# Rotary attention: scores as plain float32 products of 64 rows in the two row halves of the array

## The reference

```python
qkv = xn @ w_qkv                                   # xn: twice normalized x, (2, 1024, 128)
q, k, v = heads(q), heads(k), heads(v)             # (2, 16, 1024, 64)
q = concat([q[:, :, :1], rope(q[:, :, 1:])])       # rope(t) = t * cos + rot(t) * sin
k = concat([k[:, :, :1], rope(k[:, :, 1:])])
dots = einsum('bhqd,bhkd->bhqk', q, k) * 64 ** -0.5
out = einsum('bhqk,bhkd->bhqd', softmax(dots), v)
x = x + out.reshape(2, 1024, 1024) @ w_out
```

## Time and profile before

| | us |
|---|---|
| median of 3 runs | 1244.94 (1240.4 to 1246.34) |
| profiled execution, device time | 1243.7 |
| its span, first to last instruction | 1241.8 |
| row maxima of the rotary attention, first to last start | 36.6 to 721.7 |
| mean granted TensorE clock | 0.926 of 2.4 GHz |

### The profile page before, as it was taken

How to read it: one execution, slowest core, us unless ns; L and a number is a source line. 1 busy time by engine, 2 the same in 40 slices (tenths; PEclk the granted TensorE clock), 3 DMA queues, 4 the chain that set the end, 5 groups by cost and what they waited for, 6 DMA issues and landing times. The chain is left out here.

```text
span 1241.8 us, 33787 instructions
## 1 busy us (share of the span) xinstructions
PE 1087.8 (88%) x13139; PEld 724.9 (58%) x13139; DVE 920.9 (74%) x1385; ACT 765.4 (62%) x1393; POOL 508.5 (41%) x299
## 2 busy tenths in 40 slices
PE   3799999999999999999999975937999999999876
PEld 1466666666666666666666664935744555445434
DVE  6888888888888889888888964445866665567326
ACT  4577777677777767777777736523256555456633
POOL 0466865675586567658656705730000000000000
PEclk8899999999999999999999985968589988889986
DMA  5866566555656655565666524122451110110001
GB/s 159 212 152 153 141 142 146 140 137 127 156 140 137 146 146 141 123 154 135 137 146 152 138 87 141 53 73 94 145 180 43 53 53 18 36 53 19 2 7 34
DMA packets 63338, 138.14 MB, mean 111 GB/s; under 512 B 12737, under 2 KB 33122, under 8 KB 59186
## 3 DMA queue, kind: packets, MB, share of 16 engines
q1 hardware_dynamic: 61426, 132.87, 42.1%
q0 software_dynamic: 1856, 4.52, 1.2%
HBM read 62.77 MB, written 22.41 MB: 69 GB/s over the span
## 5 line engine op out<-in xcount | busy, mean ns | idle before, releaser
L566 ACT ACTIVATE a_probs<-a_score,a_negmax 128x1024 f32<-128x1024 f32 x256 | 285.5, 1115 | 185.3 <-DVE a_negmax L668 182.6
L668 DVE TENSOR_REDUCE a_negmax<-a_score 128x1 f32<-128x1024 f32 x256 | 310.0, 1211 | 91.5 <-PE a_score L444 91.5
L1586 DVE TENSOR_REDUCE a_lowest<-a_score 128x1 f32<-128x512 f32 (+3 forms) x320 | 181.7, 629 | 84.3 <-PE a_score L1474 46.7
L1556 ACT ACTIVATE a_probs_T<-a_score_T 128x1024 f32<-128x1024 f32 (+1 forms) x192 | 146.7, 810 | 136.9 <-PE a_score_T L1450 93.9
L674 DVE STREAM_TRANSPOSE a_probs_Tb<-a_probs 128x1024 f32<-128x1024 f32 x128 | 156.9, 1226 | 0.1
L674 DVE STREAM_TRANSPOSE a_probs_Ta<-a_probs 128x1024 f32<-128x1024 f32 x128 | 156.9, 1226 | 0.0
L401 POOL TENSOR_TENSOR residual<-residual,a_scaled 128x512 f32<-128x512 f32 x62 | 79.3, 1290 | 146.3 <-ACT a_scaled L582 146.3
L444 PE MATMUL a_score<-a_k_stackbh,a_q_stackb 128*128 128x512 f32 x256 | 113.6, 444 | 25.1 <-ACT a_probs L566 25.1
L444 PE MATMUL a_score<-a_k_stackah,a_q_stacka 128*128 128x512 f32 x256 | 119.3, 466 | 17.1 <-DMA a_q_stacka<-a_q_lo 14.5
L456 PE MATMUL a_acc<-a_probs_Tb,a_v_repb 32*64 32x256 f32 x4096 | 127.8, 384 | 2.3 <-ACT a_scaled L582 2.3
L456 PE MATMUL a_acc<-a_probs_Ta,a_v_repa 32*64 32x256 f32 x4096 | 126.9, 380 | 0.0
(11 more groups left out here) (248 smaller groups left out, 1886.8 us busy)
## 6 DMA issues: line engine op xcount, KB each, us to landing
shared<-shared SPq DMA_DIRECT2D x136, 128.0 KB, 2.3
a_v_repa<-rows_v SPq DMA_DIRECT2D x64, 256.0 KB, 4.5
a_v_repb<-rows_v SPq DMA_DIRECT2D x64, 256.0 KB, 5.0
a_xn_cur<-normed_T SPq DMA_DIRECT2D x17, 512.0 KB, 3.4
rows_v<-a_v_stage SPq DMA_DIRECT2D x68, 128.0 KB, 2.4
a_k_stackah<-a_k_stackah SPq DMA_DIRECT2D x16, 256.0 KB, 2.9
a_k_stackal<-a_k_stackal SPq DMA_DIRECT2D x16, 256.0 KB, 2.9
a_q_stacka<-a_q_lo SPq DMA_DIRECT2D x16, 256.0 KB, 2.9
```

The costliest lines, as they stand in the source:

```text
L566: nc.scalar.activation(probs[s % 2][:], score_ps[s % 2][:], ACT.Exp, bias=negmax[:, s:s + 1], accum_out=den[:, s:s + 1]).then_inc(probs_re ...
L668: nc.vector.tensor_reduce(negmax[:, s:s + 1], score_ps[s % 2][:], axis=AX.X, op=ALU.max, negate=True)\
L1556: nc.scalar.activation(probs_T[k % 4][:, 2 * hp:2 * hp + 2, 0:hi - lo], score_T_ps[n % 2][:, :, 0:hi - lo], ACT.Exp).then_inc(pair_free, 1)
L1586: nc.vector.tensor_reduce(to, src, axis=AX.X, op=ALU.max, negate=True).then_inc(bank_free, 1)
```

## The change

The split is gone. q and k are used as the plain float32 that `total` leaves in `turned`:

- `q_twice[h]` holds the 64 rows of head h in both halves of the partitions; `k_halves[h]` holds keys 0 to 511 in partitions 0 to 63 and keys 512 to 1023 in partitions 64 to 127. SyncE places both by four DMAs for each head (`place`), straight from `turned`.
- A score tile is two float32 products of 64 rows and 512 columns. Each uses one row half of the array and writes its own PSUM bank.
- `high_part` and `rest` are removed, and with them two ScalarE and two GpSimd instructions for each head, and those of ScalarE and VectorE ahead of the loop.
- `total` now waits until both heads' operands of the pair before have been placed. `place_next(h, pairs)` waits for both totals, and through `rden_ready[h]` for the end of head h's scores. `rden_ready` is split by head.
- GpSimd's loop has a new order: both `add_group`s, both `scale`s, both `total`s.

```diff
-        q_lo = sb("q_lo", [P, N], F32R)
-        q_stack = [sb(f"q_stack{h}", [P, N], F32R) for h in "ab"]
-        k_stack = [[sb(f"k_stack{h}{part}", [P, N], F32R) for part in ("h", "l")] for h in "ab"]
+        q_twice = [sb(f"q_twice{h}", [P, N]) for h in "ab"]
+        k_halves = [sb(f"k_halves{h}", [P, N // 2]) for h in "ab"]
...
+                def place(h, i):
+                    own = slice(64 * h, 64 * h + 64)
+                    for c in range(2):
+                        to, cols = (q_twice[h], slice(0, N)) if i == 0 else (k_halves[h], slice(c * N // 2, c * N // 2 + N // 2))
+                        sp.dma_start(to[64 * c:64 * c + 64, :], turned[i][own, cols]).then_inc(operands_placed[h], 16)
...
-                def stack(h, pairs):
-                    sp.wait_ge(hi_ready[h][1], pairs)
-                    copy_rows(k_stack[h][0], k_stack[h][0], h)
-                    sp.wait_ge(lo_ready[h][1], pairs)
-                    copy_rows(k_stack[h][1], k_stack[h][1], h)
-                    sp.wait_ge(lo_ready[h][0], pairs)
-                    copy_rows(q_stack[h], q_lo, h)
+                def place_next(h, pairs):
+                    sp.wait_ge(summed[0], pairs)
+                    sp.wait_ge(summed[1], pairs)
+                    sp.wait_ge(rden_ready[h], pairs)
+                    for i in range(2):
+                        place(h, i)
...
                 def total(i, p):
                     pool.wait_ge(rotated[i], count(p, 2, 2))
+                    for h in range(2):
+                        pool.wait_ge(operands_placed[h], count(p, PLACED, 0))
                     nc.gpsimd.tensor_tensor(turned[i][:], raw[i][:], rot[i][:], ALU.add).then_inc(summed[i], 1)
...
-                        now, p, later = (it, 0), (it, 1), (it, 2)
-                        pool.wait_ge(summed[1], count(p, 1, 1))
+                        now, later = (it, 0), (it, 2)
                         pool.wait_ge(added, count(now, 4, 2))
-                        for i in (1, 0):
-                            rest(0, i, p)
-                        pool.wait_ge(lo_ready[0][0], count(p, 1, 1))
                         add_group(0, now, batch)
-                        scale(0, later)
-                        pool.wait_ge(rotated[0], count(later, 2, 2))
-                        for i in (1, 0):
-                            rest(1, i, p)
-                        pool.wait_ge(lo_ready[1][0], count(p, 1, 1))
-                        total(0, later)
-                        scale(1, later)
-                        total(1, later)
                         add_group(1, now, batch)
+                        for i in range(2):
+                            scale(i, later)
+                        for i in range(2):
+                            total(i, later)
...
                     for half in range(2):
-                        cols = slice(half * 512, half * 512 + 512)
-                        for part in range(2):
-                            last = nc.tensor.matmul(score_ps[s % 2][:, cols], q_stack[h][:, tile * P:tile * P + P],
-                                                    k_stack[h][part][:, cols], start=part == 0, stop=part == 1)
+                        rows = slice(64 * half, 64 * half + 64)
+                        last = nc.tensor.matmul(score_ps[s % 2][:, half * 512:half * 512 + 512], q_twice[h][rows, tile * P:tile * P + P],
+                                                k_halves[h][rows, :], start=True, stop=True)
...
                         if s == TB - 1:
-                            pe.wait_ge(stacked[1], count(p, STACKED, STACKED))
+                            pe.wait_ge(operands_placed[1], count(p, PLACED, PLACED))
                         if s == SLOTS - 1:
-                            pe.wait_ge(stacked[0], count(p, STACKED, 2 * STACKED))
+                            pe.wait_ge(operands_placed[0], count(p, PLACED, 2 * PLACED))
...
-                    if s in (10, 11) and not last:
-                        i = 11 - s
-                        act.wait_ge(summed[i], count(p, 1, 2))
-                        act.wait_ge(scores_ready, count(p, SLOTS, TB))
-                        high_part(0, i)
-                    if s in (1, 2) and not (first or tail):
-                        act.wait_ge(scores_ready, count(p, SLOTS, 0))
-                        high_part(1, 2 - s)
```

More of the change, by code:

```diff
@@ L195, in rotary_attention @@
         summed = [sem("q_summed"), sem("k_summed")]
-        hi_ready = [[sem(f"{n}_hi_{h}_ready") for n in "qk"] for h in "ab"]
-        lo_ready = [[sem(f"{n}_lo_{h}_ready") for n in "qk"] for h in "ab"]
-        stacked = [sem("a_stacked"), sem("b_stacked")]
+        operands_placed = [sem("a_operands_placed"), sem("b_operands_placed")]
         v_stored, v_loaded = sem("v_stored"), [sem("v_a_loaded"), sem("v_b_loaded")]
@@ L201, in rotary_attention @@
         item_ready, item_kept = sem("item_ready"), sem("item_kept")
-        pv_done, attn_kept, rden_ready, projected, out_kept, added = (sem(n) for n in ("pv_done", "attn_kept", "rden_ready", "projected", "out_kept", "added"))
-        STACKED, V_PARTS, ITEMS = 48, 64, 6
+        pv_done, attn_kept, projected, out_kept, added = (sem(n) for n in ("pv_done", "attn_kept", "projected", "out_kept", "added"))
+        rden_ready = [sem("rden_a_ready"), sem("rden_b_ready")]
+        PLACED, V_PARTS, ITEMS = 64, 64, 6
         ITEM_SLOTS = {14: (2, (0,)), 15: (2, (1,)), 0: (1, (2, 3)), 6: (1, (4,)), 7: (1, (5,))}
@@ L255, in load_wo @@
                         sp.dma_start(wo_cur[h][64 * half:64 * half + 64, :], w_out[rows, :]).then_inc(wo_loaded[h], 16)
-                def copy_rows(to, src, h):
-                    own, other = slice(64 * h, 64 * h + 64), slice(64 - 64 * h, 128 - 64 * h)
-                    sp.dma_start(to[other, :].bitcast(F32), src[own, :].bitcast(F32)).then_inc(stacked[h], 16)
+                def place(h, i):
[3 more added lines that the diff above has]
+                        sp.dma_start(to[64 * c:64 * c + 64, :], turned[i][own, cols]).then_inc(operands_placed[h], 16)
                 def store_v(rows):
@@ L299, in _ @@
                 load_weights(slice(P, 2 * P))
-                stack(0, 1)
-                stack(1, 1)
+                for i in range(2):
+                    sp.wait_ge(summed[i], 1)
+                    place(0, i)
+                for i in range(2):
+                    place(1, i)
                 sp.wait_ge(item_kept, ITEMS)
@@ L325, in _ @@
                     q_kept, k_kept, v_kept = (count(q, ITEMS, k) for k in (2, 4, 6))
-                    stack(0, pairs)
+                    place_next(0, pairs)
                     sp.wait_ge(pv_done, a_valued)
@@ L337, in _ @@
                     swap_halves(1)
-                    stack(1, pairs)
+                    place_next(1, pairs)
                     sp.wait_ge(pv_done, b_valued)
@@ L386, in total @@
                     pool.wait_ge(rotated[i], count(p, 2, 2))
+                    for h in range(2):
+                        pool.wait_ge(operands_placed[h], count(p, PLACED, 0))
                     nc.gpsimd.tensor_tensor(turned[i][:], raw[i][:], rot[i][:], ALU.add).then_inc(summed[i], 1)
-                def rest(h, i, p):
-                    rows = slice(64 * h, 64 * h + 64)
-                    pool.wait_ge(hi_ready[h][i], count(p, 1, 1))
-                    nc.gpsimd.tensor_tensor((q_lo, k_stack[h][1])[i][rows, :], turned[i][rows, :], (q_stack[h], k_stack[h][0])[i][rows, :].bitcast(F32),
-                                            ALU.subtract).then_inc(lo_ready[h][i], 1)
                 def add_group(h, p, batch):
@@ L546, in _ @@
                 pe.wait_ge(item_kept, 4)
-                pe.wait_ge(stacked[0], STACKED)
+                pe.wait_ge(operands_placed[0], PLACED)
                 scores(0)
@@ L567, in exponentials @@
                                          accum_out=den[:, s:s + 1]).then_inc(probs_ready, 1)
-                def high_part(h, i):
-                    rows = slice(64 * h, 64 * h + 64)
-                    nc.scalar.activation((q_stack[h], k_stack[h][0])[i][rows, :], turned[i][rows, :], ACT.Copy).then_inc(hi_ready[h][i], 1)
                 def keep_attention():
@@ L651, in _ @@
                     keep_item(k, first_bank(k))
-                for i in range(2):
-                    act.wait_ge(summed[i], 1)
-                    for h in range(2):
-                        high_part(h, i)
                 act.wait_ge(negmax_ready, 1)
@@ L736, in _ @@
                     rotate_first(i)
-                for h in range(2):
-                    rows = slice(64 * h, 64 * h + 64)
-                    for i, to, high in ((1, k_stack[h][1], k_stack[h][0]), (0, q_lo, q_stack[h])):
-                        dve.wait_ge(hi_ready[h][i], 1)
-                        nc.vector.tensor_tensor(to[rows, :], turned[i][rows, :], high[rows, :].bitcast(F32), ALU.subtract).then_inc(lo_ready[h][i], 1)
                 dve.wait_ge(scores_ready, 1)
```

11 lines of the change are left out of this document (7 added, 4 removed).

## The result

| | before | changed |
|---|---|---|
| median, same chip, 4 runs each | 1243.63 us | 1323.49 us (1321.4 to 1333.55) |
| ratio, 95% interval | 1 | 1.0659 (1.0598 to 1.072) |
| profiled execution, span | 1243.7, 1241.8 | 1324.14, 1322.3 |
| first row maximum starts | 36.63 | 33.55 |
| loop, first to last row maximum | 685.1 | 776.6 |

The period is the distance of the first row maxima of two pairs. The time is 6.6% longer, 20 us above the point of 1303 and inside the range of 1270 to 1345. The loop is 91.5 us longer: 14 x 6.15 = 86.1 in pairs 1 to 14, 1.7 in pair 0, 3.7 in the last.

The account below looks back on a forecast made before the run. VectorE and TensorE were both taken as close to the bound. Profiled 1243.7 + 48 (stall) + 14 (clock) - 3.8 (ahead of the loop) = 1301.9; the median lies 1.2 above that execution, so 1303 us, range 1270 to 1345.

Parts of the forecast that it names:

- The mechanism: TensorE in slot 15: a stall of about 3.4 us that carries through every pair, 48 us over 14 pairs; chance 0.80.
- Score tile: Scores on TensorE: two float32 products side by side take 1.05 us, 0.07 less a tile.
- The rival of halves not side by side: Score products on TensorE: row halves don't overlap fully, tile 1.48 us, program about 1350 to 1358; chance 0.08.
- Stretch to slot 7: From a pair's first scores to slot 7's scaling end: 26.76 us, change taken as zero, bounds -0.6 and +0.7.
- The count of seven: TensorE, from a pair's first scores to slot 7: seven switches of tile shape, +0.7 us together.
- the price of 0.1: TensorE, between scores and neighbours of another tile shape: each switch estimated at about 0.1 us.
- GpSimd: GpSimd behind slot 7's scaling: one add and six long instructions, totals ready 15.5 us later.
- Placing: SyncE's four DMAs behind the totals: issues 1.45, landing 2.9, semaphores 0.1, together 4.45 us; bounds 3.85 and 6.55.
- The range's high end: Likeliest case over 14 pairs: 14 x (3.4 + 0.7 + 1.2 + 1.0) = 88, so 1329; 1354 with the clock at its bound.
- Clock: TensorE around slot 15's stall: falls to 1.2 GHz cost 1.0 us a pair, bounds 0 and 2.8; 14 us in all.
- the rival's place: Slots 8 to 10, only scores left: clock falls again after the stall's fall; 1328 and more, to 1365; chance 0.08.
- Ahead of the loop: Between k's total and the first scores: about 3.1 us where 6.9 were, saving 3.8 us.

Follow-up runs that it names:

- Experiment 1: Changed kernel with GpSimd adding head b's rows behind the rotation again, as before the change; ratio 1.0105 to the kernel before.
- experiment 2: Changed kernel with q's two copies issued when q's total is done, not when both totals are; ratio 1.0253 to the kernel before.
- experiment 9: Changed kernel, its GpSimd order kept, with rounded float32r operands and the rounding rest left out of the scores; ratio 1.0438 to the kernel before.
- experiment 4: Kernel of experiment 1 with both score products reading rows 0 to 63, keys 512 to 1023 left out; 1510.56 us, one run.
- experiment 3: Changed kernel with four float32 filler products of 128x512 ahead of TensorE's wait in slot 15; ratio 1.0558 to the kernel before.
- experiment 5: Kernel of experiment 1 with rounded float32r operands, the rounding rest left out of the scores; median 1192.85 us, ratio 0.9481 to the kernel before.

## Why the prediction held, and what it missed

The mechanism was the forecast's: TensorE stalls in slot 15 of pairs 1 to 14, on the placing's DMA, behind a chain over GpSimd that hangs on slot 7. Experiment 1 removes it by order alone, experiment 2 shortens it and gets its length back, experiment 9 shows that TensorE's own work has no part in the chain, 15.31 + 5.63 with a shorter tile; it has a part in the stretch ahead of it. Its points in turn:

- *Score tile.* 1.05 predicted, 1.06 measured. The rival of halves not side by side is out: experiment 4 shows what one row half costs (1.91).
- *Stretch to slot 7.* 26.76 predicted as unchanged (-0.6 to +0.7), 27.07 at full clock. The shorter tiles did not pay for the changes of form. The count of seven was right; the price of 0.1 and the saving of 0.07 were not. I had shared the 0.2 that a chunk of values takes beyond its streams between its two ends, but the neighbour has as much, so a change costs about 0.2; and next to an item the old tile took 1.01, not 1.12. Slot 7 got 0.33 longer where my terms give 2 x 0.1 - 0.07 = 0.13. Over a pair it comes to 0.55 us (43.85 against 43.29).
- *GpSimd.* 15.5 predicted, 15.28 measured. The stall that followed is 3.4 us predicted and 3.5 on average (48.7 in 14 waits).
- *Placing.* This is the term that was mis-sized: 4.45 predicted, 5.64 measured (mean; the median is 5.65), with bounds of 3.85 to 6.55. The last issue started 1.83 behind the first (313.20 against 311.37) where I took 1.45, and its copy landed 3.68 behind its start (316.88) where I took 2.9, the landing of the old copies. Experiment 2, with q's two copies out of the way, needs 3.31 from total to scores. 1.19 us in each of 14 pairs is 17 us. The range's high end had room for just that: it counted 1.2 for this term, though the term's own bound lay 2.1 above.
- *Clock.* 1.0 us a pair predicted (0 to 2.8), 1.39 to 1.46 measured (49.44 against 48.06 with filler, or 47.98 in pairs without one behind the stall). A fall came behind nine of the 14 stalls, so it was right that not every stall need bring one. Another 0.36 a pair comes from falls behind the slots with scores only once the stall is gone (44.21 against 43.85), so the rival's place was real, though not its size (whose 1365 should read 1367: 1303 + 14 x 4.6). By the rule of the Trainium skill ("TensorE: Matmul & The Clock Gate", "Why this matters for your kernels") that gaps in TensorE's work cost the fast clock, the term would lie nearer the upper bound of 2.8; it came out above my 1.0, but in the middle. The traces agree with the rule by the length of the gap: the nine waits of 4.03 us and more had a fall behind them, the five of 2.40 to 2.47 had none.
- *Ahead of the loop.* From the end of k's total to the first scores 3.1 predicted, 3.03 measured; but the total itself ended 0.75 later, so the first maximum came 3.1 earlier, not 3.8.
- *The pairs at the ends.* Pair 0 and the last one were left out of the sum; they got 1.7 and 3.7 longer. The last one's is the clock behind the last stall: with the filler of experiment 3 it is 3.4 shorter.

Together, against the prediction's own sum: stretch +0.31, GpSimd -0.22, placing +1.19 and clock +0.46, 1.74 a pair or 24 us; ends of the loop +5.4; ahead of it +0.7; behind it -8.0; before's own time -1.3. That is 21, where the median lies 20.5 above 1303. The part behind the loop has the same program in both; in the kernels on the first experiments' chip it took 534 to 538 us, so it differs by chip and by run. I did not settle what it depends on. So the loop was 29 us longer than the prediction has it, and that the total is off by 20.5 only is luck, from the part behind it.

The experiments found no version with full float32 scores that beats the kernel before. The nearest, experiment 1, is 1.1% above it. The rounded one of experiment 5 beats both.

## What to carry to other kernels

When a step is moved behind a wait, add up the whole chain from what releases the wait to what needs the result, its DMA issues and landings included, and compare it with the free time between those two points; a shorter product between those two points gains nothing while that chain is the longer one. Count the borders between tile forms on TensorE, not the tiles: a change that makes a product shorter but unlike its neighbours can lose it again. And put what nobody waits for, here the second addition, last in its turn.

## What the hardware showed that I had not expected

- Four copies of 64 rows, issued in a row on one queue (768 KB), slow each other down: the first issue takes 0.51 us and the last 1.24, the first copy lands 2.98 us behind the start of its issue and the others 3.7 (at 314.35, 315.63, 316.26, 316.88). k's two, issued 1.7 us behind q's in experiment 2, land after 2.6 and 2.7. The Trainium skill ("DMA: Bandwidth & Descriptors", "Rules for kernel authors") says that transfers to two partition halves serialize. That the copies land in turn doesn't show it, for their issues start 0.56 to 0.64 us apart as well; the one us more that k's need behind q's is in keeping with it.
- A product of 8 columns costs 0.21 us ahead of scores of its own form, and 0.32 with 128 rows ahead of the same scores.
- A stall of 4.05 us in slot 15 (and each of the other eight as long) was followed by a fall, here of 5.7 us at 1.2 GHz, in which TensorE was busy for 5.68 (the window at 316.90); the five stalls of 2.4 us were not, nor those of 1.7 in experiment 2. A filler ahead of the wait kept the clock at 1.00 and left a gap of 0.62. The clock also fell without any such stall, behind two slots with scores only.
